# A graph network on one core: three of TensorE's signals given from a drain instead of from the group's last product

## The chip, the core and the metric

The kernel runs on one core of a Trainium2 chip. The metric is the device time in microseconds (us). A core has TensorE (PE in the profile; its weight loads are PEld), VectorE (DVE), ScalarE (ACT), GpSimd (POOL) and SyncE (SP, which here only issues DMAs). Engines run on their own and meet at semaphores: an instruction adds to one when it is through, another waits until it has reached a number. SBUF is the working memory, PSUM (the array `banks`, eight banks) is what TensorE writes.

## What is computed

Four layers over a graph of 6,250 nodes with 96 features and 106,250 edges, sorted by their destination. After each layer the input is added and the rows are normalised.

```
L0: twice: leaky_relu(segment_max(x[src] @ W_msg + edge_attr @ W_edge, dst) + x @ W_root + b)
L1: relu(x @ Ws.T + bs + segment_sum((relu(edge_attr @ W1.T + b1) @ W2.T + b2) * x[src], dst) @ Wn.T + bn)
L2: twice: segment_sum(norm[:, None] * h[src], dst)
L3: segment_sum((x * out_deg**-0.5)[src], dst) @ weight * in_deg**-0.5 + bias
x = layernorm(x + layer(x)) after each of the four
```

## The kernel before

The work has two parts. **Three passes over the edges** (p = 0, 1 for the two convolutions of L0, p = 2 for L1) gather a row for each edge. The branch of the code that runs is the second one (`pe.Else`, lines 928 on), since the edges come sorted. **Three dense hops** (line 1112 on) then multiply with an adjacency matrix that passes 1 and 2 have built on the side. Between passes stands `nodes(p)`, work over the nodes.

A pass goes over 26 pairs of chunks, each of eight quarters (k = 0 to 7) of 512 edges: 208 quarters a pass, 624 in all, written out without a loop on the engines. A quarter goes so:

- GpSimd gathers its rows with four indirect DMAs (L709) into one of eight places of `gath`. Before it fills a place again it waits for `s_turn` (passes 0, 1) or `s_msg` (pass 2) of the quarter that lay there.
- TensorE turns the four tiles of rows into columns of a PSUM bank (L976) and, in passes 0 and 1, adds the edge features' products (L981). Then `s_turn` is raised. In pass 2 VectorE has multiplied the rows first (L1813, `msg_now`), with the products of two more groups, `hidden` (L947) and `edge_rows` (L956).
- VectorE runs the segmented maximum or sum as a scan along the 512 columns (L1831). It waits for `s_turn` of its quarter and then raises `s_scan`.
- TensorE turns the scanned columns back, two quarters later (`LAG = 2`, L995), and `s_back` is raised. It needs `s_scan` of that quarter, and `s_evac` for the bank.
- ScalarE copies them out (L1332), waiting for `s_back`, raises `s_evac` and issues the store.

Pass 0 also counts edges by node: VectorE makes one-hot tiles (L1483, L1485; `s_hot`), TensorE multiplies them (L1007; `s_hist`). In passes 1 and 2 TensorE makes windows of the adjacency matrix from other one-hots (L1022; `s_window_mm`), which ScalarE copies out (L1350).

There is no scheduler: every engine works off its instructions in the order in which they are written. On TensorE a quarter is, in pass 0, turn back (L995), count (L1007), turn (L976, L981); in pass 1 turn back, windows (L1022), turn; in pass 2 hidden, edge rows, turn back, windows, turn. There are two banks each for what is turned and for what is turned back, so `turn` of a quarter also waits for the scan two quarters before.

Who waits for the three signals: `s_turn`: VectorE's scan, GpSimd's gather (passes 0, 1), SyncE's loads of edge features, VectorE's message (pass 2). `s_back`: ScalarE's copy, and the scan at the start of a chunk. `s_hist`: VectorE's one-hots, two quarters later.

Of the kernel before, what the change touches and what calls it, by code (L numbers as in the profile page):

```python
# [89 lines left out]
def gnn_kernel(nc, x_nodes, x_t, src_t, dst_t, dst_now, dst_before, ea17_t, ea32_t, ea17_rows, ea32_rows,  # L90
# [29 lines left out]
    with ctx:  # L120
# [3 lines left out]
        def sem(name, at=None):  # L124
            return (at or ctx).enter_context(nc.semaphore(name))
# [186 lines left out]
        s_turn = sem("s_turn")  # L312
        s_scan = sem("s_scan")
        s_back = sem("s_back")
# [4 lines left out]
        s_hist = sem("s_hist")  # L319
# [100 lines left out]
        def pair_loaded(p, i):  # L420

            return PAIRS // 2 * p + i // 2 + 1
# [305 lines left out]
        def _(pe):  # L728
# [80 lines left out]
            with pe.If(is_general > 0):  # L809
                pe.wait_ge(s_y[0], GROUPS)  # L810
                with pe.Fori(0, QUARTERS) as q:
                    pe.wait_ge(o_hot, q + 1)
                    for t in range(QT):
                        m = pe.matmul(hist_ps, hot_lo[:, 0, 0, t, :], hot_hi[:, 0, 0, t, :], start=t == 0, stop=t == QT - 1)
# [16 lines left out]
                for p in range(PASSES):  # L831
# [33 lines left out]
                    def turn(i, k):  # L865

                        if KIND[p] == PLAIN:
                            pe.wait_ge(s_gath[k], 16 * QT * (PAIRS * p + i + 1))
                        else:
                            pe.wait_ge(s_msg, base + 8 * i + k + 1)  # L870
                        if not under(i, k, 2):
                            pe.wait_ge(s_scan, base + 8 * i + k - 1)
                        for t in range(QT):
                            if KIND[p] == PLAIN:
                                rows_in = gath[:, k // 4, QT * (k % 4) + t, :]
                            else:
                                rows_in = msg[:, k % 2, t * D:(t + 1) * D]
                            m = pe.transpose(turn_ps[k % 2][:, t * P:(t + 1) * P], rows_in, ident[:, :])
                        m.then_inc(s_turn, 1)
# [54 lines left out]
            with pe.Else():  # L934
                settle()
                for p in range(SPARSE):
# [23 lines left out]
                    def turn(i, k):  # L960

                        b = k // 4
                        if KIND[p] == EDGE32 and k == 0:
                            pe.wait_ge(s_ea[i % 2], 16 * pair_loaded(p, i))
                        if KIND[p] == EDGE17:
                            pe.wait_ge(s_msg, 8 * i + k + 1)
                        else:
                            pe.wait_ge(s_gath[k], 16 * QT * (PAIRS * p + i + 1))
                        if not under(i, k, 2):
                            pe.wait_ge(s_scan, base + 8 * i + k - 1)  # L970
                        for t in range(QT):
                            if KIND[p] == EDGE17:
                                rows_in = msg_now[:, k % 2, t * D:(t + 1) * D]
                            else:
                                rows_in = gath[:, b, QT * (k % 4) + t, :]
                            m = pe.matmul(turn_ps[k % 2][:, t * P:(t + 1) * P], rows_in,  # L976
                                          ident[:, :], start=t == 0, stop=KIND[p] == EDGE17 and t == QT - 1,
                                          is_transpose=True, skip_group_check=True)
                        if KIND[p] == EDGE32:
                            columns, weights = edge_columns(i, k)  # L980
                            m = pe.matmul(turn_ps[k % 2], weights(p), columns, start=False, stop=True,  # L981
                                          skip_group_check=True)
                        m.then_inc(s_turn, 1)

                    def turn_back(i, k, first):

                        if first and k < LAG:
                            return
                        g8 = (k - LAG) % 8
                        b, g = g8 // 4, g8 % 4  # L990
                        pe.wait_ge(s_scan, base + 8 * i + k - LAG + 1)
                        if not (first and k < LAG + 2):
                            pe.wait_ge(s_evac, base + 8 * i + k - LAG - 1)
                        for t in range(QT):
                            m = pe.transpose(back_ps[g8 % 2][:, t * D:(t + 1) * D],  # L995
                                             scan[0:D, b, Q * g + t:Q * (g + 1):QT], ident[0:D, 0:D])
                        m.then_inc(s_back, 1)

                    def count(i, k, first, last):

                        if p > 0 or (first and k < 2):
                            return
                        h = k % 2
                        pe.wait_ge(s_hot, 8 * i + k - 1)
                        for s in (0, 1):
                            for t in range(QT):
                                m = pe.matmul(hists_ps[s], hot_lo[:, h, s, t, :], hot_hi[:, h, s, t, :],  # L1007
                                              start=first and k == 2 and t == 0, stop=last and k == 1 and t == QT - 1,
                                              skip_group_check=True)
                        m.then_inc(s_hist, 1)  # L1010

                    def count_windows(i, k):

# [1011 lines left out]
```

## Time and profile before

| | |
|---|---|
| median of 3 runs | 5110.67 us (5105.8 to 5115.91) |
| the profiled execution | 5120.4 us, its span 5118.6 us |
| edges, pass 0 | from 92 to 1287 us |
| edges, pass 1 | from 1452 to 2655 us |
| edges, pass 2 | from 2773 to 4108 us |
| dense hops | from 4215 us to the end |
| TensorE busy, of the span | 79% |
| GpSimd busy, of the span | 50% |
| VectorE, ScalarE busy | 44%, 20% |

The share of busy time is an average over stages that differ. The views to read are the busy times by stretch, the waits, and the instructions in order of time. In a timeline a row is a run of like instructions: its start, its length, engine, line, what it writes and reads, how many, and in brackets how long the engine had been idle before it and what ended that. Lengths of TensorE's products are modelled, and runs overlap a little. A releaser "remote" or "another core or an unknown queue" is one for which the view found a semaphore's update but no instruction that had just ended and could have made it. There is one core here.

### The profile page before, as it was taken

How to read it: one execution, taken by the hardware profiler on the slowest of the kernel's cores; microseconds unless marked ns; L12 is line 12 of the kernel's file. 1: busy time of each engine (PE TensorE's matmuls, PEld its weight loads, DVE VectorE, ACT ScalarE, POOL GpSimd, SP SyncE). 2: the span in 40 equal slices, each digit the busy share in tenths (PEclk: the TensorE clock that was granted, in tenths of full speed). 3: DMA queues.
4: the chain of work that ended last, by engine and by line, in shares of the span. 5: the costliest groups of instructions: out<-in, count | busy, mean ns of one | idle time of the engine just before them, and what ended most of it. 6: DMA issues, size and time to landing. Idle time of an engine off the chain costs nothing.

```text
span 5118.6 us, 56111 instructions
## 1 busy us (share of the span) xinstructions
PE 4044.6 (79%) x19316; PEld 2656.8 (52%) x19316; DVE 2232.8 (44%) x5877; ACT 1002.8 (20%) x2108; POOL 2581.0 (50%) x2689
## 2 busy tenths in 40 slices
PE   5777767677368776777764998998898969999999
PEld 4333333333333333333333655555555649999999
DVE  3454555555124444444443555555555552222211
ACT  1100000000122222222223333333333330001101
POOL 4666666665556666666655665566566530000000
PEclk9999999999965667666655566556666559999999
DMA  5333333333234444444432443434343327777776
GB/s 136 100 99 89 102 95 100 89 101 88 48 93 136 124 135 127 137 121 138 131 100 66 117 122 114 123 115 123 110 127 108 117 84 268 269 266 268 263 260 219
DMA packets 251432, 695.04 MB, mean 136 GB/s; under 512 B 80458, under 2 KB 163082, under 8 KB 219914
## 3 DMA queue, kind: packets, MB, share of 16 engines
q1 hardware_dynamic: 56126, 348.35, 21.2%
q0 software_dynamic: 85568, 131.83, 12.0%
q10 hardware_dynamic: 109516, 212.06, 11.4%
q8 instruction: 119, 1.95, 0.2%
q14 instruction: 103, 0.84, 0.1%
HBM read 477.94 MB, written 214.09 MB: 135 GB/s over the span
## 4 chain that ended last, share of the span: by engine, by line
PE 59%; another core or an unknown queue 14%; DVE 12%; issue 10%; ACT 2%; DMA 1%; POOL 1%; DVEq 0%; ACTq 0%; POOLq 0%; SPq 0%
PE banks L1118 17%; PE banks L981 9%; PE banks L1022 7%; PE banks L976 6%; PE banks L956 6%; PE banks L947 5%; PE banks L995 5%; DVE scan L1831 5%; DVE hot_lo L1483 3%; DVE hot_hi L1485 1%; PE banks L735 1%; DVE hot_key L1848 1%; DVE hot_src L1850 1%; ACT adj L1350 1%
## 5 line engine op out<-in xcount | busy, mean ns | idle before, releaser
L709 POOL DMA_INDIRECT gath<-table,ids x2496 | 2406.3, 964 | 1425.4 <-issue 698.5
L1831 DVE TENSOR_TENSOR_SCAN scan<-keep_of,scan,banks 96x512 f32<-96x512 bf16 x621 | 791.3, 1274 | 1737.9 <-remote 972.9
L1118 PE MATMUL banks<-r_parts,adj_in 128*128 128x288 bf16 x7203 | 890.2, 286 | 5.1 <-DVE r_parts L1531 2.6
L1118 PEld LDWEIGHTS banks<-r_parts,adj_in 128*128 128x128 bf16 x7203 | 883.2, 142 | 7.4 <-DVE r_parts L1531 3.4
L995 PEld LDWEIGHTS banks<-ident,scan 96*128 96x128 f32 x2496 | 400.9, 224 | 911.7 <-issue 505.7
L995 PE MATMUL banks<-ident,scan 96*128 96x96 f32 x2496 | 528.4, 359 | 325.7 <-DVE scan L1831 254.5
L981 PE MATMUL banks<-ea_of,w_edge_of 32*96 32x512 f32 x832 | 765.1, 1016 | 0.3 <-issue 0.3
L1022 PE MATMUL banks<-hot_key,hot_src 128*128 128x392 bf16 x1600 | 543.3, 475 | 272.8 <-issue 139.3
L1332 ACT ACTIVATE back<-banks 128x384 f32<-128x384 f32 x624 | 305.2, 489 | 2062.0 <-remote 873.4
L1848 DVE TENSOR_SCALAR hot_key<-iota_key,key_t 128x392 bf16<-128x392 int16 x1600 | 505.4, 316 | 21.0 <-ACT key_t L1371 21.0
L956 PEld LDWEIGHTS banks<-w_edge_out,hid 97*128 97x128 f32 x1664 | 320.2, 287 | 307.2 <-issue 305.4
L1350 ACT ACTIVATE adj<-banks 128x392 bf16<-128x392 f32 x800 | 380.1, 496 | 431.2 <-remote 198.1
L976 PE MATMUL banks<-ident,gath 128*96 128x128 f32 x1664 | 421.5, 405 | 37.6 <-ACT r_sb L1155 21.1
L947 PE MATMUL banks<-ea_of,w_edge_of 32*96 32x512 f32 x416 | 359.4, 958 | 98.5 <-ACT hid L1320 68.6
L1022 PEld LDWEIGHTS banks<-hot_key,hot_src 128*128 128x128 bf16 x1600 | 194.3, 131 | 433.9 <-issue 413.4
L1850 DVE TENSOR_SCALAR hot_src<-iota_b,key_t 128x128 bf16<-128x128 bf16 x1600 | 397.3, 248 | 0.0
L956 PE MATMUL banks<-w_edge_out,hid 97*128 97x96 f32 x1664 | 364.7, 389 | 35.2 <-DVE msg_now L1813 29.8
L976 PEld LDWEIGHTS banks<-ident,gath 128*96 128x96 f32 x1664 | 288.0, 188 | 99.5 <-issue 28.7
L652 POOL DMA_INDIRECT agg<-scanned_rows,end_ix x150 | 145.7, 972 | 179.6 <-DMA scanned_rows<-back 74.0
L1320 ACT ACTIVATE hid<-banks,w_edge_in_b 96x512 f32<-96x512 f32 x208 | 141.9, 682 | 469.1 <-remote 209.5
L981 PEld LDWEIGHTS banks<-ea_of,w_edge_of 32*96 32x96 f32 x832 | 153.1, 239 | 140.7 <-issue 140.7
L1938 DVE TENSOR_REDUCE v<-banks 128x288 f32<-128x864 f32 (+1 forms) x34 | 34.8, 1022 | 399.2 <-PE banks L1118 399.2
(158 smaller groups left out, 2100.9 us busy)
## 6 DMA issues: line engine op xcount, KB each, us to landing
adj_in<-adjacency SPq DMA_DIRECT2D x147, 1568.0 KB
scanned_rows<-back ACTq DMA_DIRECT2D x153, 768.0 KB
adjacency<-adj ACTq DMA_DIRECT2D x100, 784.0 KB
gath<-table,ids POOLq DMA_INDIRECT x2496
ea_of<-in_ea_t SPq DMA_DIRECT2D x78, 512.0 KB
keep_of<-keep_max_d SPq DMA_DIRECT2D x52, 768.0 KB
keep_of<-keep_sum_d SPq DMA_DIRECT2D x26, 768.0 KB
table<-x_sb SPq DMA_DIRECT2D x10, 240.0 KB, 4.4
```

The costliest lines, as they stand in the source:

```text
L709: pool.indirect_dma_start(gath[:, b, t, :], None, tables[p][:, :], bass.IndirectOffsetOnAxis(ap=ids[:, 1, n:n + 1], axis=0),).then_inc(s_g ...
L947: pe.matmul(hid1_ps, weights(2), columns, start=True, stop=True)\
L956: m = pe.matmul(w1_ps[:, t * D:(t + 1) * D], hid[:, k % 2, t * P:(t + 1) * P], W["edge_out"][:, :], start=True, stop=True)
L976: m = pe.matmul(turn_ps[k % 2][:, t * P:(t + 1) * P], rows_in, ident[:, :], start=t == 0, stop=KIND[p] == EDGE17 and t == QT - 1, is_trans ...
L981: m = pe.matmul(turn_ps[k % 2], weights(p), columns, start=False, stop=True, skip_group_check=True)
L995: m = pe.transpose(back_ps[g8 % 2][:, t * D:(t + 1) * D], scan[0:D, b, Q * g + t:Q * (g + 1):QT], ident[0:D, 0:D])
L1022: m = pe.matmul(window_ps[j], hot_src[:, 2 * (k % 2) + j, a, :], hot_key[:, 2 * (k % 2) + j, a, :], start=a == 0, stop=a == KEY_TILES - 1)
L1118: m = pe.matmul(sum_ps[:, u, j, :], adj_in[:, a, :, h], r_parts[:, n % 2, h, :, :].rearrange("p k f -> p (k f)"), start=h == 0, stop=h == ...
L1350: act.activation(adj[:, half, at:at + WINDOW, :].rearrange("p d h -> p (d h)"), window_ps[j], ACT.Copy)\
L1831: ve.tensor_tensor_scan(scan[0:D, b, at:at + Q], keep_of[:, i % 2, CHUNK * b + at:CHUNK * b + at + Q], turn_ps[k % 2], start, keep_op, tak ...
L1848: ve.tensor_scalar(hot_key[:, h, a, :], iota_key[:, :], key_t[:, 0, a, bass.ds(n, 1)], None, ALU.is_equal)
L1850: last = ve.tensor_scalar(hot_src[:, h, a, :], iota_b[:, :], key_t[:, 1, a, bass.ds(n, 1)], None, ALU.is_equal)
```

## The change

At three places the signal of a group of products moves off the group's last product. A `drain` is put behind the group on TensorE, and the drain raises the semaphore. A drain computes nothing: the engine goes on to its next instruction once all before it is through. The other signals of TensorE (`s_hid_ps`, `s_w`, `s_window_mm`, those of `nodes` and of the dense hops) stay on the last product. No instruction changes its place; 624 drains come in for `s_turn`, 624 for `s_back` and 208 for `s_hist`, 1,456 in all.

```
 columns, weights = edge_columns(i, k)
 m = pe.matmul(turn_ps[k % 2], weights(p), columns, start=False, stop=True,
               skip_group_check=True)
-                        m.then_inc(s_turn, 1)
+                        pe.drain().then_inc(s_turn, 1)
...
 for t in range(QT):
     m = pe.transpose(back_ps[g8 % 2][:, t * D:(t + 1) * D],
                      scan[0:D, b, Q * g + t:Q * (g + 1):QT], ident[0:D, 0:D])
-                        m.then_inc(s_back, 1)
+                        pe.drain().then_inc(s_back, 1)
...
 m = pe.matmul(hists_ps[s], hot_lo[:, h, s, t, :], hot_hi[:, h, s, t, :],
               start=first and k == 2 and t == 0, stop=last and k == 1 and t == QT - 1,
               skip_group_check=True)
-                        m.then_inc(s_hist, 1)
+                        pe.drain().then_inc(s_hist, 1)
```

## Rows read from the trace of the kernel before

**Rows 1.** Busy time by stretch: start:end, length, engines (instructions), PEclk, DMA, GB/s.
```profile
92.00:1287.00 1195.00, 853.57 (x3733) 422.18 (x3732) 616.05 (x1039) 104.03 (x214) 752.06 (x797) 1.00 0.37 97
1452.00:2655.00 1203.00, 893.81 (x2864) 420.54 (x2863) 578.70 (x1799) 286.10 (x606) 792.95 (x813) 0.62 0.43 127
2773.00:4108.00 1335.00, 1192.14 (x4496) 736.35 (x4494) 683.87 (x2011) 417.75 (x810) 791.70 (x814) 0.61 0.39 114
```
**Rows 2.** GpSimd's gathers by line, passes 0, 1 and 2: busy, mean ns, idle before.
```profile
L709 POOL DMA_INDIRECT gath<-table,ids x797 | 752.3, 944 | 414.6 <-issue 218.1 <-remote 106.1 <-PE banks L981 90.5
...
L709 POOL DMA_INDIRECT gath<-table,ids x813 | 793.8, 976 | 388.5 <-issue 229.2 <-remote 145.4 <-PE banks L981 14.0
...
L709 POOL DMA_INDIRECT gath<-table,ids x814 | 791.7, 973 | 512.5 <-DVE msg_now L1813 281.9 <-issue 230.5
```
**Rows 3.** Waits of the whole span: us in total, times, longest.
```profile
DVE scan L1831 <- remote: 973.9, 150, 14.7
```
**Rows 4.** Pass 0 in order of time: TensorE alone.
```profile
698.79 2.02 PE L981 MATMUL banks<-ea_of,w_edge_of 32*96 32x512 f32 x2
...
702.81 2.02 PE L981 MATMUL banks<-ea_of,w_edge_of 32*96 32x512 f32 x2
...
709.33 0.92 PE L995 MATMUL banks<-ident,scan 96*128 96x96 f32 x4 [4.50 <-DVE scan L1831]
...
712.39 2.02 PE L981 MATMUL banks<-ea_of,w_edge_of 32*96 32x512 f32 x2
714.34 0.92 PE L995 MATMUL banks<-ident,scan 96*128 96x96 f32 x4
715.05 0.54 PE L1007 MATMUL banks<-hot_hi,hot_lo 128*128 128x50 bf16 x8
715.42 1.07 PE L976 MATMUL banks<-ident,gath 128*96 128x128 f32 x4
716.42 2.02 PE L981 MATMUL banks<-ea_of,w_edge_of 32*96 32x512 f32 x2
718.37 0.92 PE L995 MATMUL banks<-ident,scan 96*128 96x96 f32 x4
```
**Rows 5.** The same stretch: who waits for TensorE's signals.
```profile
708.00 1.28 DVE L1831 TENSOR_TENSOR_SCAN scan<-keep_of,scan,banks 96x512 f32<-96x512 bf16 x1 [6.95 <-remote]
708.05 0.49 ACT L1332 ACTIVATE back<-banks 128x384 f32<-128x384 f32 x1 [7.46 <-remote]
708.17 0.94 POOL L709 DMA_INDIRECT gath<-table,ids  x1 [2.96 <-remote]
...
710.28 0.49 ACT L1332 ACTIVATE back<-banks 128x384 f32<-128x384 f32 x1 [1.75 <-PE banks L995]
...
710.92 1.27 DVE L1831 TENSOR_TENSOR_SCAN scan<-keep_of,scan,banks 96x512 f32<-96x512 bf16 x1
```
**Rows 6.** The last product of the kernel, its drain, and who waits.
```profile
5113.68 0.74 PE L1102 MATMUL banks<-w_l,node_t 97*128 97x96 f32 x2 [4.28 <-ACT node_t L1439]
5114.46 0.26 DVE L1975 TENSOR_TENSOR v<-banks,x_sb 128x96 f32<-128x96 f32 x1 [2.84 <-PE banks L1102]
...
L120 PEldq DRAIN  x1: 790/790/790, 5113.7 to 5113.7; - x1
```
**Rows 7.** Elsewhere in order of time: ScalarE's copy and the group that waits for it.
```profile
133.65 0.38 ACT L1361 ACTIVATE key_lines<-banks 128x256 f32<-128x256 f32 x1 [9.87 <-PE banks L1034]
...
134.09 0.47 PE L1034 MATMUL banks<-ident,flag 128*128 128x128 f32 x1 [0.47 <-ACT key_lines L1361]
```
**Rows 8.** Pass 2, TensorE: a group at either clock, and the two stretches' busy times.
```profile
3309.26 2.02 PE L947 MATMUL banks<-ea_of,w_edge_of 32*96 32x512 f32 x2
...
3315.49 1.09 PE L947 MATMUL banks<-ea_of,w_edge_of 32*96 32x512 f32 x2
...
3299.00:3314.00 15.00, 15.00 (x54) 9.62 (x54) 7.09 (x22) 4.09 (x9) 7.20 (x8) 0.50 0.30 73
3316.00:3322.00 6.00, 6.00 (x38) 3.99 (x36) 3.15 (x10) 2.02 (x4) 4.59 (x5) 1.00 0.97 317
```

More of the change, by code:

```diff
@@ L982, in turn @@
                                           skip_group_check=True)
-                        m.then_inc(s_turn, 1)
+                        pe.drain().then_inc(s_turn, 1)
                     def turn_back(i, k, first):
@@ L996, in turn_back @@
                                              scan[0:D, b, Q * g + t:Q * (g + 1):QT], ident[0:D, 0:D])
-                        m.then_inc(s_back, 1)
+                        pe.drain().then_inc(s_back, 1)
                     def count(i, k, first, last):
@@ L1009, in count @@
                                               skip_group_check=True)
-                        m.then_inc(s_hist, 1)
+                        pe.drain().then_inc(s_hist, 1)
                     def count_windows(i, k):
```

## The prediction, made before the result was known

> **What bounds the kernel now.** I read the busy times by stretch first. In the edge passes no engine is full: in pass 0 (1195 us) TensorE is busy 854 us and GpSimd 752, in pass 1 (1203 us) 894 and 793, in pass 2 (1335 us) 1192 and 792 [rows 1]. In the dense hops TensorE is full, and the change touches nothing there. So the question is who stands idle in the passes, and for what. The waits say: VectorE's scan waited 974 us, in 150 waits, for "remote" [rows 3], an update of a semaphore that no instruction had just made. On one core that means an update that came long after its instruction.
>
> The timeline of pass 0 shows it. The group that turns a quarter ends at 698.79 + 2.02 = 700.81. TensorE goes on; the next turning ends at 702.81 + 2.02 = 704.83, and then it is idle 4.5 us [rows 4]. Everyone else stands too: the scan starts at 708.00, ScalarE's copy at 708.05, GpSimd's gather at 708.17, all after "remote" [rows 5]. Which scan is it? TensorE turns a quarter only after the scan of two quarters before; the scan that follows the group ending at 714.41 (712.39 + 2.02) is one more, and between them stands the scan at 710.92. Counted back, 710.92 belongs to the group that ended at 704.83 and 708.00 to the one that ended at 700.81. Its signal took 7.2 us, in which TensorE went through its whole next quarter and then stood. After the idle time signals are quick: turning back ends at 709.33 + 0.92 = 710.25 and the copy starts at 710.28 [rows 4, 5]. So the bound of passes 0 and 1, and part of pass 2, is a loop: TensorE runs ahead until it needs a scan, the scan waits for a signal of TensorE that is held back. The floors below it are TensorE's own products and GpSimd's gathers. For the gathers I take their busy time and the part of their idle time that is put down to issue, per record, times 832 a pass: pass 0 (752.3 + 218.1) / 797 x 832 = 1013 us, pass 1 (793.8 + 229.2) / 813 x 832 = 1047 us, pass 2 (791.7 + 230.5) / 814 x 832 = 1045 us [rows 2].
>
> **What the change adds.** 1,456 drains. Each costs TensorE the overlap of its group's last product with the next group, and the time to start again. The overlap is read off neighbours: turning back ends at 715.26 and the next group starts at 715.05, 0.21 us; the count ends at 715.59, next 715.42, 0.17 us; turning ends at 718.44, next 718.37, 0.07 us [rows 4]. The restart has no row of its own, since only one drain stands behind products. It begins with the kernel's last group at 5113.7 and takes 790 ns, so it ends at about 5114.5, some 0.05 to 0.1 us after the products' end at 5114.42; VectorE starts at 5114.46 on that group's own signal [rows 6]. Starting a group that waits for ScalarE takes 134.09 - (133.65 + 0.38) = 0.06 us [rows 7]. I take 0.1 us for drain and restart together, nearest to these. A quarter of pass 0 then pays 0.21 + 0.17 + 0.07 + 3 x 0.1 = 0.75 us, one of passes 1 and 2 (two drains) 0.28 + 0.2 = 0.48 us; times 208 that is 156, 100 and 100 us, 356 us of TensorE's time, 0.245 us a drain. From below, with only 0.07 us behind each and the overlaps kept, it is 102 us. From above I take 0.5 us a drain, 728 us, as an estimate: twice my value, because the next weights must be loaded and issued anew and no row shows that through a drain.
>
> **What it takes away.** If the drain's signal comes when the products are through, the 7 us holds go. Why should they? What I see is that signals are quick on short runs of products (the group before the copy at 133.65, the last one, the first after each idle time [rows 4 to 7]) and late after a long run without a stop. A drain makes every run short: four to eight products, then a stop. The Trainium skill (Perfetto Trace Analysis, "Sequencer-only Instruction (DRAIN, etc)" under "Per-engine timelines") has a drain's semaphore pushed by the sequencer when its execution ends, and a product's only when PSUM has acknowledged all bytes; no run here shows the two ways side by side. It speaks for another road of the signal, but not against a drain that waits for a late acknowledgement.
>
> Then per pass. Pass 0: TensorE 853.6 + 156 = 1010 us, gathers 1013; two engines that are equally long don't overlap perfectly, so I add 50 us: 1060 against 1195, a gain of 135. Pass 1: TensorE 893.8 + 100 = 994, gathers 1047; plus 50, 1095 against 1203, a gain of 108. Pass 2: TensorE 1192 + 100 = 1292; the 143 us in which it is idle now shrink to some 35, 1327 against 1335, a gain of 8. The sum is 251 us. The profiled execution took 5120.4 us, so 4869, and the median of the runs is 9.7 us lower: **4860 us**. In pass 2 the holds' going pays for the drains and little more, since there TensorE is the bound at 89% busy. Late next are the gathers in passes 0 and 1, and TensorE in pass 2. What is queued behind a drain is the next group, in pass 0 the count behind the turning back; who waits for that is VectorE's one-hots, two quarters on, with slack. The signals that stay on products (`s_w`, `s_hid_ps`, `s_window_mm`) lie between drains, so they too should be quick.
>
> TensorE's clock is in these numbers as it was: a `hidden` group takes 2.02 us in a stretch whose granted clock is 0.50, the 1.2 GHz level, though TensorE is busy all of it, and 1.09 us in one at 1.00, the 2.4 GHz level [rows 8]. In pass 0 the column says 1.00 while two such products (L981) take 2.02 us as at the low level [rows 1, 4], so I don't trust it there and go by lengths. Over pass 1 and 2 it was 0.62 and 0.61 [rows 1]. More stops could lower it, fewer long idle times raise it; I leave it.
>
> **Rivals.** (1) The holds stay, because what holds the signal is something that the drain waits for as well. The place is every group of the passes; the drains then add TensorE's 356 us and remove nothing: 5111 + 356 = 5467, somewhat less where a drain falls into time that is idle anyway; I call it **5400** (5290 to 5470). It decides when a drain ends later than about 0.42 us behind its group on the mean, since 251 us / 1,456 = 0.17 us is what the forecast can lose. For it: I don't know what holds the signals, and in one hold TensorE had been idle for 3 us (704.83 to 707.9) before they came [rows 4, 5], so an empty engine alone does not free them. Against it: TensorE itself never seems to wait for anything in a hold, and the holds start only after several groups in a row.
>
> (2) Signals are quick, but a drain costs some 0.5 us instead of 0.25, as the upper bound has it. Pass 0: 853.6 + 312 + 50 = 1216, pass 1: 893.8 + 208 + 50 = 1152, pass 2: 1192 + 208 + 35 = 1435: +21 - 51 + 100 = +70, **5181 us**. Drains of 0.35 to 0.5 us give 4960 to 5180. The Trainium skill (TensorE: Matmul & The Clock Gate, "Step-by-step: what each phase is for", point 5) says that the array's emptying overlaps the next product's filling, and that a product by itself cannot hide it; its constant for that at the low clock is (219)/1.2 = 183 ns. By that the drains would cost, as an estimate, 1,456 x 183 ns = 266 us, near my 356, and the forecast would be up to 90 us lower; the overlap of 0.07 to 0.21 us in rows 4 agrees with the rule in kind.
>
> (3) Drains are cheap (the 102 us) and all goes to the floors: pass 0 1013, pass 1 1047, pass 2 1192 + 29 = 1221, gains of 182, 156 and 114 us, 452 in all: **4659 us**. A higher granted clock in pass 2 would do the same.
>
> **How the numbers follow.** The forecast has a chance of 0.50, with a range of its own from 4760 to 4960; rival 3 has 0.12 (4600 to 4760); rival 2 has 0.17 (4960 to 5190), of which 0.07 is faster, 0.03 within 0.2% and 0.07 slower; rival 1 has 0.21. Faster by over 0.2%, which is about what a measurement of this kernel can tell from no change, is 0.50 + 0.12 + 0.07 = 0.69, within it 0.03, slower 0.07 + 0.21 = 0.28. The range leaves out half of rival 3 and most of rival 1: 4680 to 5300.
>
> **What would show it.** Right: "remote" is gone from the scan's waits or is a tenth of 974 us; in pass 0 TensorE repeats every 1060 / 208 = 5.1 us instead of running three quarters and standing; scans start 0.1 us behind their turning; gathers follow each other at (752.3 + 218.1) / 797 = 1.22 us without pauses; passes 0 and 1 end 135 and 108 us sooner. A drain that ends within 0.1 us of its group, and a next group that starts right then, would show the cost. Wrong: drains of microseconds in the trace (rival 1); quick signals, but gaps of 0.5 us between groups and a pass 2 of over 1400 us (rival 2); a pass 2 near 1220 us (rival 3). The forecast falls as a whole if the holds have a cause that stops on TensorE's side do not touch.

## The result: slower, and the profile after

The changed kernel takes **5356.4 us** (median of 4 runs, 5326.5 to 5370.0) against 5108.2 us for the kernel before (4 runs, 5100.9 to 5115.9): 1.048 times as long, 95% interval 1.043 to 1.053. The forecast was 4860 us, faster, with a range of 4680 to 5300. It was wrong in sign and outside its range. The time lies in the range of the prediction's own rival 1, "the holds stay" (5400 us, 5290 to 5470).

First the busy times by stretch of the changed kernel, for its three edge passes: start:end, length, then PE, PEld, DVE, ACT and POOL busy with instruction counts, PEclk, DMA share, GB/s.

```profile
92.00:1420.00 1328.00, 914.52 (x3745) 423.19 (x3745) 622.24 (x1042) 104.47 (x215) 754.36 (x798) 1.00 0.33 87
1572.00:2795.00 1223.00, 994.68 (x2851) 443.90 (x2852) 585.45 (x1797) 297.63 (x604) 814.46 (x822) 0.55 0.43 125
2937.00:4332.00 1395.00, 1273.01 (x4465) 738.70 (x4466) 683.62 (x2001) 437.90 (x807) 799.61 (x805) 0.58 0.37 109
```

Beside [rows 1], pass 0 went from 1195 to 1328 us, pass 1 from 1203 to 1223, and pass 2 from 1335 to 1395. The stretches of before were cut a little wider in pass 2 than the pass itself; from the first scan to the last it is 1300 us in a repeated run of before and 1396 in one of after (experiment 1). Nearly all of the loss is therefore in the first and the third pass, +133 and +96 us. In pass 0 TensorE is busy 61 us more and idle 72 us more (1328 - 914.5 = 413.5 against 1195 - 853.6 = 341.4).

Then the waits of the whole span: us in total, times, longest.

```profile
DVE scan L1831 <- PEq L983: 1540.4, 476, 45.4
DVE scan L1831 <- issue: 404.8, 147, 17.7
...
DVE msg_now L1813 <- remote: 19.6, 2, 17.0
```

The "remote" wait of the scan [rows 3] is gone, but only by name: the scan waits for the drain at L983 (PEq is TensorE's sequencer) in 476 waits. Did the hold go, or did it move into the drain? The timeline of TensorE and the two engines behind it in pass 0 (start us, duration us, in brackets the idle time before and what ended it) shows both kinds of quarter:

```profile
700.06 0.89 PE L995 MATMUL banks<-ident,scan 96*128 96x96 f32 x4 [0.55 <-issue]
...
701.03 0.51 PE L1007 MATMUL banks<-hot_hi,hot_lo 128*128 128x50 bf16 x8
...
704.42 1.06 PE L976 MATMUL banks<-ident,gath 128*96 128x128 f32 x4 [2.88 <-issue]
...
705.41 2.02 PE L981 MATMUL banks<-ea_of,w_edge_of 32*96 32x512 f32 x2
707.55 1.27 DVE L1831 TENSOR_TENSOR_SCAN scan<-keep_of,scan,banks 96x512 f32<-96x512 bf16 x1 [4.60 <-PEq L983]
...
707.65 0.88 PE L995 MATMUL banks<-ident,scan 96*128 96x96 f32 x4 [0.23 <-issue]
...
709.36 1.06 PE L976 MATMUL banks<-ident,gath 128*96 128x128 f32 x4 [0.23 <-issue]
...
710.35 2.02 PE L981 MATMUL banks<-ea_of,w_edge_of 32*96 32x512 f32 x2
712.49 1.27 DVE L1831 TENSOR_TENSOR_SCAN scan<-keep_of,scan,banks 96x512 f32<-96x512 bf16 x1 [1.95 <-PEq L983]
```

From 705.41 to 710.35 a quarter runs much as the forecast had it (5.1 us): 4.94 us, the scan starts 0.12 us after its turning (705.41 + 2.02 = 707.43, then 707.55), the next group 0.22 us after. In the kernel before an undisturbed quarter takes 716.42 - 712.39 = 4.03 us [rows 4], so three drains cost 0.91 us. But at 701.03 a count ends at 701.54, after only eight short products, and the next group starts 2.88 us later. TensorE stands behind its own drain. The drain rows of pass 0 (minimum, median and maximum in ns; a drain's time starts when the sequencer reaches it, so the median holds the group's own products) say the same:

```profile
L983 PEldq DRAIN  x206: 2859/3008/4107, 93.5 to 1412.6; - x103
L997 PEldq DRAIN  x208: 737/890/5524, 91.8 to 1419.6; - x104
L1010 PEldq DRAIN  x208: 488/493/6295, 92.8 to 1418.8; - x104
```

The drain of a count takes 0.49 us at the median, and up to 6.3 us. The one that stands between the count at 701.03 and the next group ends at 704.21.

No view prints how late each drain is, but the trace's records give it: a drain's end less the modelled end of its group. On time it is 0.02 us. In pass 0 of the changed kernel 97 of the 208 drains behind counts, 20 behind turnings back and 14 behind turnings are more than 0.5 us late. What stands before the end of the late ones sums to 226, 38 and 15 us, 279 us in all. In pass 1 it is 127 us, in pass 2 39 us.

### The profile page after: what moved, and what is told of

Its sections match the earlier page's. It is cut to its first block, busy times and chain, and to the rows that moved or that the text cites. A ratio compares the mean times of both kernels' runs of the same rounds, so it can differ in the third digit from the quotient of the medians.

```text
span 5349.4 us, 57567 instructions
## 1 busy us (share of the span) xinstructions
PE 4305.9 (80%) x19316; PEld 2690.5 (50%) x19316; DVE 2250.4 (42%) x5877; ACT 1038.1 (19%) x2108; POOL 2612.1 (49%) x2689
## 4 chain that ended last, share of the span: by engine, by line
issue 38%; PEld 25%; PE 18%; PEldq 12%; another core or an unknown queue 2%; DVE 2%; DMA 1%; ACT 1%; POOL 1%; DVEq 0%; ACTq 0%; POOLq 0%; SPq 0%
PE banks L1118 16%; PEld banks L976 8%; PEldq L997 7%; PEld banks L995 6%; PEld banks L956 5%; PEldq L983 4%; PEld banks L981 3%; PEld banks L1022 2%; PEld banks L1007 1%; PE banks L735 1%; PEld banks L947 1%; PEldq L970 1%; POOL agg L652 1%; DVE scan L1831 0%
## 5 line engine op out<-in xcount | busy, mean ns | idle before, releaser
L709 POOL DMA_INDIRECT gath<-table,ids x2496 | 2437.6, 977 | 1608.4 <-issue 633.3
L981 PE MATMUL banks<-ea_of,w_edge_of 32*96 32x512 f32 x832 | 804.7, 1066 | 0.0
L1022 PE MATMUL banks<-hot_key,hot_src 128*128 128x392 bf16 x1600 | 574.9, 512 | 179.6 <-issue 151.8
L976 PE MATMUL banks<-ident,gath 128*96 128x128 f32 x1664 | 434.0, 414 | 298.3 <-issue 276.2
L1350 ACT ACTIVATE adj<-banks 128x392 bf16<-128x392 f32 x800 | 396.2, 497 | 338.0 <-PE banks L1022 252.2
L947 PE MATMUL banks<-ea_of,w_edge_of 32*96 32x512 f32 x416 | 358.0, 955 | 56.8 <-issue 22.7
L1022 PEld LDWEIGHTS banks<-hot_key,hot_src 128*128 128x128 bf16 x1600 | 171.0, 125 | 413.2 <-issue 379.1
L976 PE MATMUL banks<-ident,msg_now 128*96 128x128 f32 x832 | 218.2, 415 | 1.9 <-DVE msg_now L1813 1.7
```

The lines of the kernel that those rows point to most:

```text
L709: pool.indirect_dma_start(gath[:, b, t, :], None, tables[p][:, :], bass.IndirectOffsetOnAxis(ap=ids[:, 1, n:n + 1], axis=0),).then_inc(s_g ...
L947: pe.matmul(hid1_ps, weights(2), columns, start=True, stop=True)\
L1022: m = pe.matmul(window_ps[j], hot_src[:, 2 * (k % 2) + j, a, :], hot_key[:, 2 * (k % 2) + j, a, :], start=a == 0, stop=a == KEY_TILES - 1)
L1350: act.activation(adj[:, half, at:at + WINDOW, :].rearrange("p d h -> p (d h)"), window_ps[j], ACT.Copy)\
```

## The experiments

Kernels that share a job ran on one chip, beside shared runs of the kernel before. That kernel took 5067 to 5117 us in the first comparison and in three jobs, and 4445 and 4448 us in two others (chips recorded as 14, 0 and 5, and 13 and 5), all its runs within a job being alike. So each measurement below is read against its own job's time, and the difference between the jobs is a finding of its own (last section).

**Experiment 1: both kernels again.** Job with before at 5106.0 us; no edit.

> The kernel before, profiled again. Theory A (late signals belong to the chip or its condition, not to the kernel): the time falls in one of two classes, near 5110 us with VectorE's scan waiting some 970 us for 'remote', or near 4448 us with no such waits and passes of 1032, 1058 and 1048 us. Theory B (they belong to the kernel and come and go from run to run): both in one call.

> The change again. Where there are no late signals: drains end within 0.05 us of their group, the gathers hold passes 0 and 1 as they do without drains, pass 2 pays; 1.01 to 1.02 of the kernel before (the run with drains and signals on products gave 1.0155). Where there are late signals: 1.043 to 1.053, as in the first comparison, and drains that end late.

Measured 5115.0 us (ratio 1.001) and 5347.1 us (1.047, 1.044 to 1.050). The same stretches, first scan to last scan of each pass, of before and then of after:

```profile
90.00:1290.00 1200.00, 857.03 (x3741) 423.27 (x3740) 617.79 (x1038) 103.78 (x214) 755.10 (x800) 1.00 0.36 96
1454.00:2660.00 1206.00, 912.95 (x2871) 423.44 (x2870) 580.90 (x1800) 286.70 (x607) 796.59 (x813) 0.63 0.43 127
2808.00:4108.00 1300.00, 1182.39 (x4496) 735.81 (x4496) 688.49 (x2007) 419.17 (x812) 769.44 (x792) 0.61 0.40 117
```

```profile
91.00:1415.00 1324.00, 916.95 (x3740) 424.01 (x3740) 623.09 (x1039) 103.98 (x214) 756.09 (x800) 1.00 0.33 87
1582.00:2807.00 1225.00, 1006.74 (x2869) 449.21 (x2869) 586.95 (x1800) 299.19 (x606) 792.49 (x814) 0.55 0.43 125
2949.00:4345.00 1396.00, 1288.21 (x4514) 748.59 (x4514) 689.58 (x2007) 440.16 (x812) 785.55 (x796) 0.58 0.37 109
```

The passes cost +124, +19 and +96 us, 239 in all; the spans differ by 237 us (5345.5 against 5108.4). The loss is fully in the passes, and it repeats.

**Experiment 2: one drain at a time, where signals are not late.** In each kernel the drain replaces the product's signal in one group alone; in the fourth the signals stay where they were and the drains stand behind them.

```diff
 e1_turn   -m.then_inc(s_turn, 1)   +pe.drain().then_inc(s_turn, 1)
 e1_back   -m.then_inc(s_back, 1)   +pe.drain().then_inc(s_back, 1)
 e1_hist   -m.then_inc(s_hist, 1)   +pe.drain().then_inc(s_hist, 1)
 e1_both    m.then_inc(...)         +pe.drain()      (all three groups)
```

> Only s_turn from a drain (624 drains). Theory A: a stop of 0.07 + 0.06 to 0.21 us each, 150 us in sum, part of it in idle time, but the runs between stops stay long in passes 1 and 2: 1.00 to 1.02, most in pass 2. If short runs shorten the holds (my forecast's mechanism): under 0.99.

> Only s_back from a drain (624 drains). Theory A: 0.21 us of overlap and 0.06 to 0.21 us to start again, 260 us in sum, of which passes 1 and 2 show most: 1.015 to 1.035. If short runs shorten the holds: under 0.99.

> Only s_hist from a drain (208 drains, pass 0). Theory A with holds (in the changed kernel's trace the drains behind the counts ended 227 us late in sum): pass 0 longer by 60 to 130 us, passes 1 and 2 unchanged, 1.015 to 1.025. Rival (plain stops only, 0.38 us each, hidden where TensorE would wait anyway): within 1.00 to 1.01.

> The three signals stay on the group's last product and the 1,456 drains stand behind them, raising nothing. Theory A (a drain ends when the products' own signal would have come, so the signal's road is nothing and what costs is that TensorE stops): as the change, 1.04 to 1.055 of the kernel before, and each drain ends within 0.05 us of the product's signal, held ones too. Theory B (the drain's signal is itself slower than a product's, and that delay costs): clearly under the change, 1.02 or less.

The kernel before took 4448.2 us in this job, 13% less than I had ever seen it take. The turning back alone gave 1.001 (0.998 to 1.004), the count alone 0.998 (0.996 to 1.000), all drains behind unchanged signals 1.016 (1.012 to 1.019). The turning alone is inconclusive: its runs lay from 4432 to 4640 us and gave no ratio. The count was run again in the last job:

> Only the counts are signalled from a drain; they run in pass 0 alone. On a chip where the kernel before takes about 5100 us: if the three lines add up, 1.047 less 0.0158 and 0.0203 is left, 1.008 to 1.014, 5145 to 5185 us, all of it in pass 0. If the lines hide one another: within 0.3% of the kernel before.

There too the kernel before took 4444.7 us, and the ratio was 1.000 (0.998 to 1.002). I had wanted it where signals are late; so the count's own share there is not measured. What the scan waits for in this last run:

```profile
DVE scan L1831 <- PE banks L981: 908.1, 358, 28.1
...
```

There is no "remote" row for the scan, though this kernel signals turned rows from the product as before. The traces of the four kernels of the first job have none either. Its passes:

```profile
70.00:1103.00 1033.00, 872.72 (x3737) 443.17 (x3737) 622.53 (x1038) 103.69 (x214) 762.51 (x807) 1.00 0.43 113
1226.00:2283.00 1057.00, 810.70 (x2869) 391.98 (x2868) 586.68 (x1802) 277.55 (x607) 800.42 (x819) 0.67 0.49 145
2397.00:3448.00 1051.00, 994.38 (x4515) 631.70 (x4514) 695.47 (x2006) 411.49 (x811) 785.00 (x806) 0.73 0.50 145
```

1033, 1057 and 1051 us: the floors that the prediction worked out for the gathers (1013, 1047, 1045 us from [rows 2]) within 2%. With all three drains behind (e1_both) pass 0 takes 1063 us; the forecast for a pass 0 without holds was 1060:

```profile
71.00:1134.00 1063.00, 917.68 (x3740) 424.04 (x3740) 622.97 (x1038) 103.90 (x214) 763.28 (x807) 1.00 0.42 110
```

The other two passes of e1_both take 1058 and 1073 us. Against the run with the count's drain alone, which is from the other job, all three drains add 30, 1 and 22 us. So without late signals there is nothing for a drain to win, and most of the drains' price lies under the gathers. The kernel before has no trace of its own in such a job; the run at ratio 1.000 stands for it.

**Experiment 3: no gathers, both kernels.** The job of experiment 1, on the chip with late signals. The gathered buffer holds ones and GpSimd only raises the semaphore, so the messages are left out.

```diff
-for t in range(QT * k, QT * k + QT):
-    pool.indirect_dma_start(gath[:, b, t, :], None, tables[p][:, :], ...).then_inc(s_gath[4 * b + k], 16)
+pool.sem_inc(s_gath[4 * b + k], 64)
```

> The kernel before without the 2,496 gathers of the passes: GpSimd fills gath once with ones and raises the gathers' semaphores itself, so the edge messages are not the reference's. If signals are late: theory C (GpSimd's gathers hold them back) expects no 'remote' waits left and pass 0 near TensorE's own 4.03 us x 208 = 838 us; theory D (nothing to do with the gathers) expects them to stay. If signals are not late, it gives TensorE's own pace: pass 0 840 us.

> The same without gathers, with the drains. TensorE is then the bound, and the drains' whole price shows in pass 0: 0.45 us of overlap and 0.06 + 0.21 + 0.21 us to start again, 0.93 us a quarter, 193 us over 840. My prediction's 0.75 us a quarter would give 156 us.

Measured 3879.2 us for the kernel before without gathers and 4290.4 us for the changed one, 1.106 times as long. Pass 0 of each, and the drain of a count in the changed one's pass 0:

```profile
69.00:928.00 859.00, 837.09 (x3741) 430.78 (x3740) 622.60 (x1038) 103.92 (x214) 0.00 (x0) 1.00 0.29 89
```

```profile
70.00:1119.00 1049.00, 915.80 (x3736) 422.79 (x3736) 622.47 (x1038) 103.92 (x214) 0.00 (x0) 1.00 0.24 73
...
L1007 PEldq DRAIN  x207: 462/492/493, 74.3 to 1118.3; - x104
```

Three things follow. With no gathers no drain is late: 493 ns at most behind a count, against 6295, and read one by one all 1,456 end 0.02 us behind their group. The kernel before without gathers has no "remote" row for the scan, in the same job in which the whole kernel before waits 1077.9 us for it. Here, too, stands the drains' clean price in pass 0: 190 us, 0.91 us a quarter, of which 79 us is overlap lost (TensorE busy 837 to 916 us) and 111 us is standing between groups. The products kept their lengths in this pass (1110 ns for one of L978 in both).

The third is that the ratio of 1.106 is not the drains' price alone. Passes 1 and 2, of the kernel before and then of the changed one, both without gathers:

```profile
1096.00:1838.00 742.00, 687.95 (x2870) 362.25 (x2869) 567.34 (x1800) 270.78 (x607) 0.00 (x0) 0.81 0.45 153
1962.00:2886.00 924.00, 896.51 (x4518) 577.60 (x4516) 676.10 (x2007) 405.41 (x811) 0.00 (x0) 0.83 0.38 122
```

```profile
1283.00:2009.00 726.00, 630.68 (x2869) 329.99 (x2869) 574.78 (x1800) 274.64 (x606) 0.00 (x0) 0.97 0.46 156
2128.00:3280.00 1152.00, 1083.98 (x4517) 650.72 (x4516) 679.66 (x2007) 429.49 (x811) 0.00 (x0) 0.70 0.29 98
```

With the drains pass 1 is 16 us shorter, at a granted clock of 0.97 against 0.81, and pass 2 is 228 us longer, at 0.70 against 0.83. So outside pass 0 products that are longer or shorter at another clock lie over what a drain costs, and these runs give no clean price for it.

**Experiment 4: what in the gathers does it?** Another job, before at 5067.4 us. All four are the kernel before with another load in the place of a gather; the messages come out as other numbers in all of them.

```diff
 e3_thin   -gath[:, b, t, :], None, tables[p][:, :],
           +gath[:, b, t, 0:24], None, tables[p].rearrange('n (a f) -> (n a) f', f=24),
 e3_plain  -pool.indirect_dma_start(gath[:, b, t, :], None, tables[p][:, :], IndirectOffsetOnAxis(...))
           +pool.dma_start(gath[:, b, t, :], tables[p][P * (n % NT):P * (n % NT) + P, :])
 e3_comp   -pool.indirect_dma_start(...)                      (x4 a quarter)
           +pool.memset(busy[:, :], 1.0); pool.drain()        (x4 a quarter, then sem_inc 64)
 e3_hw     -pool.indirect_dma_start(...)
           +sp.dma_start(gath[:, b, t, :], tables[p][P * (n % NT):P * (n % NT) + P, :])
```

> The kernel before, but each gather moves 24 of a row's 96 floats (the rest of the gathered buffer holds ones), so the messages are wrong; the number of gathers and every wait stay. Theory A, signals of TensorE are late when GpSimd issues gathers, whatever they move: VectorE's scan still waits over 800 us on 'remote' in the whole run, passes stay at 1150 to 1210 us (first two). Theory B, it goes by the bytes that land in SBUF: a quarter of the bytes, the 'remote' waits fall under 400 us and the first two passes to 1035 to 1100 us.

> The kernel before, but GpSimd issues plain loads of 128 neighbouring rows in place of gathers by index: same bytes, same number, other rows, so the messages are wrong. If it is only gathers by index that come with late signals of TensorE: no 'remote' waits, and the passes go down to what GpSimd's issuing takes or to the 742 to 924 us of the run without gathers. If it is any transfer that GpSimd issues, or any traffic into SBUF: 'remote' over 800 us, passes 1150 us and more.

> The kernel before with no gathers in the passes: GpSimd fills a buffer of 128 by 896 floats of its own and drains, four times a quarter, and then raises the gather's semaphore itself; the gathered buffer holds ones, so the messages are wrong. If GpSimd's being busy (or its share of SBUF's port with VectorE) is enough for late signals: 'remote' over 500 us and passes over 1100 us. If it takes transfers: no 'remote' row among VectorE's waits, passes of 860 to 1000 us.

> The kernel before, but SyncE issues plain loads of 128 neighbouring rows from its own queue in place of GpSimd's gathers; GpSimd stands idle in the passes, the same bytes land in the same buffer; other rows, so the messages are wrong. If traffic into SBUF from any queue makes TensorE's signals late: 'remote' over 500 us. If it takes GpSimd as the issuer: no 'remote' row, and passes near the 859, 742 and 924 us of the run without gathers, unless SyncE's issuing itself is slower (over 1000 us by its own row).

Measured: a quarter of the bytes 5072.1 us (1.001, 0.999 to 1.003); plain loads issued by GpSimd 4063.8 us; GpSimd busy with fills 4327.5 us; plain loads from SyncE's queue 4045.2 us. The scan's waits with a quarter of the bytes, and then with plain loads from GpSimd:

```profile
DVE scan L1833 <- remote: 816.2, 140, 20.3
DVE scan L1833 <- PE banks L983: 511.7, 139, 44.7
```

```profile
DVE scan L1829 <- PE banks L979: 567.3, 275, 27.9
...
```

"Remote" stays with a quarter of the bytes and goes in the three others: not the bytes, not a transfer that GpSimd issues, not a busy GpSimd, not traffic into SBUF as such. What is left is the gather by index. Each costs GpSimd 965 ns here against 562 ns for the plain load, so how often they are issued differs as well. One expectation was missed on the side: with the fills pass 2 takes 1174 us, not 860 to 1000.

**Experiment 5: the split where signals are late.** Before at 5117.4 us; the kernels of experiment 2.

> Only the rows turned are signalled from a drain (one of the change's three lines). On a chip where the kernel before takes about 5100 us: if each drain waits through its group's late end and pays its stop, this line's share is about a third to a half of the whole +240 us, so 5180 to 5230 us, ratio 1.015 to 1.025. If the whole loss sits in this line (it is the one VectorE's scan waits for): 5300 us or more. If the drain takes the lateness away for this one signal: under 5050 us.

> Only the rows turned back are signalled from a drain. If every drain costs its own stop: 5160 to 5220 us, ratio 1.01 to 1.022. If the loss sits in the scan's signal alone: within 0.3% of the kernel before, since ScalarE has time to spare behind the turned back rows.

> Signals stay on the last products, and the same three drains stand behind them. If the loss is TensorE's stop at each drain (its own price and the late ends that it waits through), the time is near that of the change, 5300 to 5400 us. If the loss is that the signal leaves later, it is 5100 to 5180 us. On the chip without late signals this kernel gave 1.0155 times the kernel before; if only the quick drains' price counts, 5190 us.

Measured: turned rows 5195.5 us (1.016, 1.012 to 1.019), turned back rows 5219.9 us (1.020, 1.017 to 1.024), signals on the products with drains behind 5379.7 us (1.051, 1.047 to 1.055). The last decides a question: that kernel leaves the signals where they were and loses as much as the change (1.047). It is TensorE's stop that costs, not the place of the signal. Its scan has little "remote" left (66.1 us in 15 waits). I read that as the drain waiting out the late end, so that little is left to be seen as late.

The groups of pass 0 that stand behind a drain show how long TensorE stood (busy, mean ns, then the idle time before the group and what ended it). Before, then with the drain behind the turning alone, then behind the turning back alone, then the changed kernel:

```profile
L995 PE MATMUL banks<-ident,scan 96*128 96x96 f32 x827 | 189.5, 383 | 259.5 <-DVE scan L1831 217.6 <-issue 38.1 <-ACT back L1332 3.8
L1007 PE MATMUL banks<-hot_hi,hot_lo 128*128 128x50 bf16 x1656 | 109.6, 221 | 65.6 <-DVE hot_hi L1485 51.9 <-issue 13.7
```

```profile
L995 PE MATMUL banks<-ident,scan 96*128 96x96 f32 x826 | 183.6, 376 | 340.0 <-issue 339.9
```

```profile
L1007 PE MATMUL banks<-hot_hi,hot_lo 128*128 128x50 bf16 x1656 | 106.0, 218 | 313.0 <-issue 293.1 <-DVE hot_hi L1485 13.7
```

```profile
L976 PE MATMUL banks<-ident,gath 128*96 128x128 f32 x824 | 218.2, 420 | 274.7 <-issue 273.5 <-DVE scan L1831 1.1
L995 PE MATMUL banks<-ident,scan 96*128 96x96 f32 x831 | 184.5, 377 | 74.2 <-issue 74.1
L1007 PE MATMUL banks<-hot_hi,hot_lo 128*128 128x50 bf16 x1664 | 106.7, 219 | 57.3 <-issue 38.5 <-DVE hot_hi L1485 4.0
```

And the same three groups without gathers, where no drain is late:

```profile
L973 PE MATMUL banks<-ident,gath 128*96 128x128 f32 x828 | 219.1, 420 | 49.7 <-issue 49.2 <-DVE scan L1828 0.5
L992 PE MATMUL banks<-ident,scan 96*128 96x96 f32 x824 | 182.8, 376 | 59.2 <-issue 46.3 <-ACT back L1329 12.7
L1004 PE MATMUL banks<-hot_hi,hot_lo 128*128 128x50 bf16 x1656 | 106.2, 219 | 16.6
```

Taking the clean stops off gives what is left for late ends: 406.2 - 125.5 = 281 us in the changed kernel, 340.0 - 59.2 = 281 us with the drain behind the turning, 313.0 - 16.6 = 296 us with the one behind the turning back. The kernel before stands 325 us. The late ends added up drain by drain agree: 279, 281 and 297 us. So TensorE stands some 280 to 300 us in pass 0 wherever the drains are, and that comes on top of its own time. Pass 0 without gathers plus the late time gives 859 + 325 = 1184 for before (measured 1195) and 1049 + 281 = 1330 for after (measured 1328). That is an account and not a test, since nearly all of TensorE's idle time is in both sides of it. With one drain the clean stops (59.2 and 16.6 us) are paid by what late standing falls (44 and 29 us), to within 15 us, and pass 0 stays as it was (1193 and 1197 us against 1200). With three the price is 190 us against 44 us saved.

Pass 2, where TensorE is nearly full, pays with one drain as with three:

```profile
2800.00:4166.00 1366.00, 1247.16 (x4514) 766.95 (x4514) 707.20 (x2006) 428.70 (x812) 771.39 (x796) 0.58 0.38 111
```

```profile
2821.00:4208.00 1387.00, 1304.26 (x4512) 766.64 (x4512) 689.39 (x2006) 439.27 (x812) 783.32 (x796) 0.56 0.37 110
```

These are the turning alone and the turning back alone: +66 and +87 us on 1300, +96 for the whole change. They don't add up. The loss is in TensorE's busy time (+65, +122 and, for the whole change, +106 us), and the granted clock is lower: 0.61 before, then 0.58, 0.56 and 0.58. Products that have nothing to do with a drain take longer. In the changed kernel the products for the windows, whose signal is still on its product, went from 478 to 519 ns each. Those two rows, of pass 2 of before and of after:

```profile
L1022 PE MATMUL banks<-hot_key,hot_src 128*128 128x392 bf16 x800 | 268.1, 478 | 28.6 <-issue 21.2 <-ACT adj L1350 7.3
```

```profile
L1022 PE MATMUL banks<-hot_key,hot_src 128*128 128x392 bf16 x800 | 292.3, 519 | 85.4 <-issue 71.8 <-DVE hot_src L1850 13.6
```

In the traces of experiment 1 the windows' group grew from 268 to 292 us and the turning from 184 to 217; the other three groups stayed within 3 us. That is some 59 of the 106 us. The other 47 us are overlap between groups that is lost. What moves the clock is open: with all three drains and no late signals it was higher in pass 2 (0.78 against 0.73 in the run with the count's drain), and the pass lost 22 us.

**Experiment 6: hold the gathers back.** GpSimd waits for an earlier quarter's gathers to land before it issues the next quarter's: the quarter before (e4_pace, with experiment 5), or the one before that (e5_pace2, before at 4444.7 us). Quarter 0 of a pair looks at the pair before in the same way.

```diff
 e4_pace   +pool.wait_ge(s_gath[4 * b + k - 1], 16 * QT * (PAIRS * p + i + 1))
 e5_pace2  +pool.wait_ge(s_gath[4 * b + k - 2], 16 * QT * (PAIRS * p + i + 1))
```

> The kernel before, and GpSimd waits for the gathers of each quarter to land before it issues those of the next; nothing else differs. If late signals come from many gathers outstanding (a queue of descriptors that fills): VectorE's 'remote' waits fall from about 1000 us to under 300 us, and the time to 4500 to 4900 us, under both kernels. If each gather's issue brings them, whatever is outstanding: 'remote' stays over 700 us, and the time is 5080 to 5400 us, more by what GpSimd now waits for its landings.

> The kernel before, and GpSimd waits, ahead of a quarter's gathers, for those of the quarter before the last to land. If late signals need more than two quarters' gathers outstanding: VectorE's 'remote' waits under 300 us and 4500 to 4900 us, since the wait seldom stops GpSimd. If two quarters outstanding are as bad as many: 'remote' 700 us and more, within 2% of 5100 us. If the late signals went in the tighter version only because GpSimd issued less often: the same as that.

Measured 6622.2 us (1.294, 1.290 to 1.299) and 4763.7 us (1.071, 1.068 to 1.075). Waits of the first, VectorE and GpSimd:

```profile
DVE scan L1835 <- PE banks L985: 2393.2, 414, 25.8
...
POOL gath L713 <- DMA gath<-table,ids: 1599.7, 420, 10.3
```

In the tight version the scan has no "remote" row, on the chip where the kernel before takes 5117 us, but GpSimd waits 1600 us for landings and everything waits for GpSimd. The expectation named "remote under 300 us" and "4500 to 4900 us" together; the first came and the second did not. Whether the number outstanding or only the slower pace took the late signals away is open. The looser version cost 319 us in a job where no signal was late; its gathers waited 325 us for landings. It was not run where they are; if it took them away there, 4764 us would be less than 5117, and that is untested.

No version here beats both kernels.

## Why the prediction was wrong, point by point

**The bound.** Right as a place, incomplete as a cause. The loop of late signals was what bound passes 0 and 1: take it away (experiments 2 to 4) and the same passes run in 1033 and 1057 us or less. That it needs the gathers by index could not be read from the trace of before, in which they run all the time.

**The price of the drains.** The mechanism was right and the term too small. The sum had 0.75 us a quarter in pass 0; the undisturbed quarters give 4.94 - 4.03 = 0.91 us, and the run without gathers 190 us for 208 quarters. The mis-sized part is the restart. The lost overlap was 0.38 us a quarter (79 us / 208) where the sum had 0.45, but the standing was 0.53 us (111 us / 208) where it had 0.3. A drain on time ends only 0.02 us behind its group; it is the next 32-bit group that starts 0.22 us after its predecessor's end, behind the turning and behind the count. In the Trainium skill (TensorE: Matmul & The Clock Gate, "Step-by-step: what each phase is for") the array's emptying, which a product by itself can't hide, gave the prediction an estimate of 183 ns a drain; pass 0 measured 190 us / 624 = 0.30 us.

**What it takes away.** This is the step that failed: "If the drain's signal comes when the products are through, the 7 us holds go", with its reason, "A drain makes every run short". The drain's signal does not come when the products are through. The changed kernel has runs of four to eight products only, and TensorE stood 2.88 us behind a count of eight short ones (701.54 to 704.42), and up to 6.0 us before other groups of that line. In pass 0 the sum had 156 us of drains and still a gain of 135, all from the holds' going; in the changed kernel 279 us of late ends are still there, now inside the drains. The rows of before could have warned: the prediction noted itself that TensorE had been idle 3 us within a hold before the signals came [rows 4, 5], so the run's length was never what held them. That signals are quick after a pause was a pattern in a handful of rows; it was also what one sees if holds simply end and begin by something else. The Trainium skill (Perfetto Trace Analysis, "Sequencer-only Instruction (DRAIN, etc)" and "Tensor Engine Instruction (MATMUL, LD_WEIGHTS)") gives the two signals different roads. Experiment 5 now shows them side by side: signals on products with drains behind gave 1.051, signals on the drains 1.047. The road made no difference; a drain waits for the late end as everyone else does.

**Pass by pass.** Forecast -135, -108 and -8 us; measured +124, +19 and +96 (experiment 1). Rival 1 had 156, 100 and 100 us to add, 356 in all, "somewhat less where a drain falls into time that is idle anyway". The measured sum is 239 us. Pass 1 is where the drains fell into idle time: TensorE was idle 1206 - 913 = 293 us before and 218 us after. In pass 0 the larger price (190 for 156) was partly paid by 44 us less standing, and in pass 2 the clock took its part.

**Clock.** "More stops could lower it ... I leave it": it fell from 0.63 to 0.55 in pass 1 and from 0.61 to 0.58 in pass 2. In pass 2 TensorE's busy time rose by 106 us (1182 to 1288), of which 47 us are lost overlap (the prediction's 0.28 us a quarter gives 58); the rest is longer products at a lower clock. It does not always fall with drains: without gathers it rose in pass 1, from 0.81 to 0.97, and the pass got shorter. Leaving the term out had no reason in the rows, and in pass 2 it was over half of the loss.

**The check list.** The sign that "remote" is gone from the scan's waits came true and meant nothing, because the wait was renamed to "PEq L983". What decided was the other sign, "drains of microseconds in the trace". A sign by which to know a theory right has to be one that its rival would not give as well.

**Rivals 2 and 3** needed quick signals and fall with them. Rival 2's price (0.5 us a drain) is above the 0.30 us measured, rival 3's (0.07 us) below.

**The chances.** The stay of the holds had 0.21 although nothing in the profile said what causes them. A gain that rests wholly on an unexplained wait going away should not have had 0.5.

## What to carry to other kernels

A late signal is not cured by signalling from another instruction of the same engine: the drain waits for the same late completion, now with the engine standing, and each drain costs its stop besides (0.30 us here on the mean). One drain in a loop whose engine stands anyway may cost nothing (pass 0: 1193 and 1197 us against 1200), and the same drain costs where the engine is nearly full (pass 2: +66 and +87 us). Before moving a signal, find what the wait needs in order to exist, by taking neighbours away one at a time; a run with gathers left out would have told it.

## What the runs showed of the hardware

- While GpSimd issued gathers by index, TensorE's signals came late, in the hold of rows 4 and 5 by 7.2 us, and 973.9 to 1077.9 us of the scan's waits were for such signals. Drains behind TensorE's products ended up to 5.8 us late in pass 0 of the changed kernel (6295 ns against a median of 493), and about 11 us in two cases at the start of pass 1. They were on time in the same job with the gathers left out, and in another such job with plain loads from GpSimd or SyncE or fills on GpSimd in their place. A quarter of the bytes changed nothing. Why they are late is not shown.
- The same kernel took 5067 to 5117 us in some jobs and 4445 to 4448 in others, the second without late signals. A gather's time on GpSimd was the same in both (965 ns in a run of before at 5108 us, 968 ns with the count's drain at 4472 us). The chip recorded as 5 is among both, so a chip's number doesn't tell; whether it was another machine's chip, another core or another time is open.
- What the change does depends on it: 1.047 times the kernel before where signals are late; where they are not, the nearest kernel measured (drains behind unchanged signals) took 1.016 times as long.
- A TensorE drain on time ended 0.02 us behind the modelled end of its group. With a drain behind every group TensorE restarted 32-bit products 0.22 us after the group before; three drains a quarter cost 0.91 us.
- The granted clock moved with the drains, in both directions: in pass 1 from 0.63 to 0.55 with gathers and from 0.81 to 0.97 without, in pass 2 from 0.61 to 0.58 and from 0.83 to 0.70. The passes got longer or shorter with it. Why is not shown.
